# Row-wise start of a fused MLP kernel, with two roundings of h moved to GpSimd

## What is computed

```python
h = jax.nn.gelu(jnp.einsum('bnd,hd->bnh', x, fc1_w) + fc1_b, approximate=False)
shared = jnp.einsum('bnh,sh->bns', h, fc2_w) + fc2_b
We = experts_w[indices]
be = experts_b[indices]
expert_x = jnp.einsum('bnh,bph->bnp', h, We) + be[:, None, :]
x + jnp.concatenate([shared, expert_x], axis=-1)
```

## Time and profile before

| | us |
|---|---|
| median of 3 runs | 360.57 |
| lowest, highest | 360.05, 361.18 |
| profiled execution | 360.29 |
| its span | 358.1 |
| TensorE busy | 352.4 (98%) |
| VectorE busy | 260.3 (73%) |
| ScalarE busy | 246.6 (69%) |
| GpSimd busy | 235.0 (66%) |

### The profile page before, as it was taken

How to read it: one execution, slowest core, us unless ns; L and a number is a source line. 1 busy time by engine, 2 the same in 40 slices (tenths; PEclk the granted TensorE clock), 3 DMA queues, 4 the chain that set the end, 5 groups by cost and what they waited for, 6 DMA issues and landing times.

```text
span 358.1 us, 7085 instructions
## 1 busy us (share of the span) xinstructions
PE 352.4 (98%) x2383; PEld 324.2 (91%) x2383; DVE 260.3 (73%) x500; ACT 246.6 (69%) x410; POOL 235.0 (66%) x150
## 2 busy tenths in 40 slices
PE   8999999999999999999999999999999999999995
PEld 6899899999999999999999999999999999999984
DVE  1797976977859698686968869697786959844543
ACT  3794957777677686776777678677767768656640
POOL 0079977858756587765758866586865658774570
PEclk9999999999999999999999999999999999999999
DMA  8969654524324333332533324234331231312001
GB/s 197 189 148 206 144 144 131 150 78 108 112 59 136 94 90 126 89 120 66 147 97 88 113 78 128 82 94 149 90 102 57 88 98 32 117 37 90 29 31 59
DMA packets 70061, 37.53 MB, mean 105 GB/s; under 512 B 43530, under 2 KB 70026, under 8 KB 70026
## 3 DMA queue, kind: packets, MB, share of 16 engines
q1 hardware_dynamic: 69408, 36.55, 38.0%
q10 hardware_dynamic: 618, 0.53, 0.6%
HBM read 28.68 MB, written 8.39 MB: 104 GB/s over the span
## 4 chain that ended last, share of the span: by engine, by line
PE 98%; DVE 0%; ACT 0%; issue 0%; POOL 0%; POOLq 0%; DVEq 0%
PE fc_ps L1091 39%; PE acc_ps L1147 30%; PE acc_ps L1150 15%; PE fc_ps L1067 6%; PE acc_ps L1117 3%; PE fc_ps L1036 2%; PE fc_ps L1147 1%; PE tr_ps L1030 1%; PE fc_ps L1150 1%; PE fc_ps L1074 1%; DVE resid L914 0%; ACT w1t L469 0%; PE acc_ps L1030 0%; POOL ident L416 0%; POOL ident L414 0%
## 5 line engine op out<-in xcount | busy, mean ns | idle before, releaser
L390 POOL TENSOR_TENSOR ht<-gelu,ht 128x1024 fp32r<-128x1024 f32 x62 | 149.5, 2412 | 98.8 <-ACT ht L560 98.8
L1147 PE MATMUL acc_ps<-w2t,ht 128*128 128x512 f32 x464 | 168.0, 396 | 0.0
L1091 PE MATMUL fc_ps<-xt,w1t 128*128 128x256 f32 x1176 | 159.6, 283 | 0.0
L1091 PEld LDWEIGHTS fc_ps<-xt,w1t 128*128 128x128 f32 x1176 | 148.6, 189 | 5.3
L1150 PE MATMUL acc_ps<-w2t,ht 128*128 128x256 f32 x464 | 130.0, 280 | 0.0
L1147 PEld LDWEIGHTS acc_ps<-w2t,ht 128*128 128x128 f32 x464 | 87.4, 188 | 16.0 <-POOL ht L390 0.3
L1150 PEld LDWEIGHTS acc_ps<-w2t,ht 128*128 128x128 f32 x464 | 87.8, 189 | 0.0
L560 ACT ACTIVATE ht<-gelu 128x1024 fp32r<-128x1024 f32 x64 | 68.0, 1063 | 3.3
L586 ACT ACTIVATE gelu<-work,b 128x512 f32<-128x512 f32 x56 | 37.3, 715 | 26.4 <-DVE work L865 26.2
L398 POOL TENSOR_TENSOR xt<-work,xt 128x1024 fp32r<-128x1024 f32 x14 | 33.8, 2415 | 14.9 <-ACT xt L549 14.9
L865 DVE TENSOR_TENSOR work<-fc_ps,work 128x512 f32<-128x512 f32 x28 | 19.4, 691 | 22.6 <-PE fc_ps L1091 21.3
(11 more groups left out here) (70 smaller groups left out, 326.6 us busy)
## 6 DMA issues: line engine op xcount, KB each, us to landing
pieces<-in_L_cond_experts_w SPq DMA_DIRECT2D x128, 64.0 KB, 2.0
out<-resid SPq DMA_DIRECT2D x32, 256.0 KB, 3.1
pieces<-in_x SPq DMA_DIRECT2D x60, 128.0 KB, 2.9
resid<-in_x SPq DMA_DIRECT2D x15, 512.0 KB, 3.5
e_bias<-in_L_cond_experts_b SPq DMA_DIRECT2D x32, 32.0 KB, 2.8
work<-in_L_cond_fc_w SPq DMA_DIRECT2D x4, 256.0 KB, 4.4
w_piece<-in_L_cond_fc_w SPq DMA_DIRECT2D x4, 192.0 KB, 5.2
resid<-in_x SPq DMA_DIRECT2D x2, 256.0 KB, 3.5
```

The source lines that it names most:

```text
L390: nc.gpsimd.tensor_tensor(ht[:, slot, LO, :, :].rearrange("p k t -> p (k t)"), gelu[:, q % GELUS, :, :].rearrange("p k t -> p (k t)"), ht[ ...
L1091: last = nc.tensor.matmul(fc1_ps[:, dst, j * SEQ:(j + 1) * SEQ], w1t[:, w, wv, ms], xt[:, n % 2, o, xv, :], start=(fresh and j == 0 and at ...
L1147: nc.tensor.matmul(acc.rearrange("p (v o) -> p v o", v=2), ht[:, q % SLOTS, HI, j, ts], w2t[:, :, k, fc2_columns(b)], start=(k == 0), stop ...
```

## The change

Three things change, all in the first part of the program.

Order by rows. Loads of fc1_w half 0 are made by pairs of chunks (`load_w1_pair`): pair 0 half on SP's and half on ScalarE's queue, pair 1 on SP's; row 1 of x moves to ScalarE's queue, and index and fc1's bias go behind it. Transposes of x are by row (`x0_banks(b)` gives one bank with both halves of the features), those of fc1_w by pair of chunks. Chunks 0 and 1 are multiplied by row of x (`first_chunk(c, b)`, six matmuls of 256 columns): chunk 0 row 0, chunk 1 row 0, then, behind the transposes of the second pair, row 1 of both. Chunk 2 comes before the transposes of half 1, chunk 3 behind them. The copy of fc1's bias stays behind the `w1_low` of half 0.

Warm matmuls: `WARM` is 12 for 20, and the second group (10) is gone.

Rounding of h: for pairs 0 and 1 of block 0, GpSimd copies gelu to fp32r (`early_pair`, ahead of each `pair_lo`), and ScalarE's `conv_high(0)` and `conv_high(1)` go. On VectorE, `w1_low(1, *)` moves behind the first two `w2_square`, and on ScalarE `conv_chunk(1)` (a gelu) between the two `w1_high(1, *)`.

VectorE's `x0_low(b)` and `w1_low(half, l)` follow ScalarE's in the same forms and are left out below.

```diff
@@ -33,8 +33,9 @@
     GELUS = 4
+    EARLY = 2
     SLOTS = 6
-    WARM = 20
+    WARM = 12
@@ -115,13 +116,32 @@
+        def x0_row(v, b):
+            return xt0[:, :, v, b * SEQ:(b + 1) * SEQ]
+        def x0_bank(b):
+            return tr_ps[:, b, :].rearrange("p (d t) -> p d t", d=D)
+        W1_ORDER = ((0, 1), (1, 0))
+        def w1_slots(half, l, v):
+            cols = slice(2 * half * P, (2 * half + 2) * P)
+            if l == 0:
+                return w1t[:, W_A11:W_A12 + 1, v, cols]
+            return w1t[:, W_A22:W_A21 + 1:W_A21 - W_A22, v, cols]
+        def w1_rows(half, l):
+            return (acc_ps, tr_ps)[half][:, l, :].rearrange("p (d c) -> p d c", d=D)
...
         stored = [sem(f"stored{n}") for n in range(2)]
-        w1_loaded = [sem(f"w1_loaded{n}") for n in range(2)]
+        w1_loaded = [sem(f"w1_loaded{n}") for n in range(3)]
         w1p_loaded = sem("w1p_loaded")
@@ -195,6 +216,13 @@
+        def wait_h_hi(engine, q):
+            if q < EARLY:
+                engine.wait_ge(early_hi, q + 1)
+            else:
+                engine.wait_ge(h_hi, q - EARLY + 1)
@@ -261,11 +289,15 @@
-        def load_w1(queue, half):
-            ks = slice(half * HALF, (half + 1) * HALF)
-            for q in range(Q):
-                queue.dma_start(w1_in[S * q:S * (q + 1), ks, :], w1_v[q][:, ks, :])\
-                    .then_inc(w1_loaded[half], 16)
+        def load_w1_pair(queue, l, strips):
+            for q in strips:
+                queue.dma_start(w1_in[S * q:S * (q + 1), 2 * l:2 * l + 2, :],
+                                w1_v[q][:, 2 * l:2 * l + 2, :]).then_inc(w1_loaded[l], 16)
+        def load_x0(queue, b):
+            ts = slice(b * T, (b + 1) * T)
+            queue.dma_start(resid[:, 0, ts, :], x_blocks[0][:, ts, :]).then_inc(x0_loaded[b], 16)
@@ -312,12 +344,14 @@
-            for b in range(R):
-                ts = slice(b * T, (b + 1) * T)
-                sp.dma_start(resid[:, 0, ts, :], x_blocks[0][:, ts, :]).then_inc(x0_loaded[b], 16)
+            load_x0(sp, 0)
+            load_w1_pair(sp, 0, (0, 1))
+            load_w1_pair(sp, 1, range(Q))
             sp.wait_ge(x0_loaded[0], 16)
-            load_w1(sp, 1)
+            for q in range(Q):
+                sp.dma_start(w1_in[S * q:S * (q + 1), HALF:K, :], w1_v[q][:, HALF:K, :])\
+                    .then_inc(w1_loaded[2], 16)
             for q in range(Q):
@@ -384,9 +418,15 @@
+            def early_pair(q):
+                pool.wait_ge(conv_gelu, 2 * q + 2)
+                nc.gpsimd.tensor_copy(
+                    ht[:, q % SLOTS, HI, :, :].rearrange("p k t -> p (k t)"),
+                    gelu[:, q % GELUS, :, :].rearrange("p k t -> p (k t)")).then_inc(early_hi, 1)
...
                 slot = q % SLOTS
-                pool.wait_ge(h_hi, q + 1)
+                wait_h_hi(pool, q)
                 nc.gpsimd.tensor_tensor(
@@ -418,6 +458,8 @@
             for r in range(PAIRS):
+                if r < EARLY:
+                    early_pair(r)
                 pair_lo(r)
@@ -451,22 +493,14 @@
         def _(act):
...
+            def x0_high(b):
+                act.wait_ge(x0_tr, b + 1)
+                nc.scalar.activation(x0_row(HI, b), x0_bank(b), ACT.Copy).then_inc(x0_hi, 1)
+            def w1_high(half, l):
+                act.wait_ge(w1_tr, 2 * half + l + 1)
+                nc.scalar.activation(w1_slots(half, l, HI), w1_rows(half, l), ACT.Copy)\
+                    .then_inc(w1_hi, 1)
@@ -607,9 +641,10 @@
+            load_w1_pair(act, 0, (2, 3))
+            load_x0(act, 1)
             act.dma_start(index_sb[:, :], index.rearrange("(o n) -> o n", o=1))\
                 .then_inc(index_loaded, 16)
-            load_w1(act, 0)
             act.dma_start(b1_in[:, :].rearrange("k (q c) -> k q c", q=Q),
@@ -618,27 +653,25 @@
             act.wait_ge(gelu_loaded, 1)
-            for d in range(D):
-                x0_high(d)
-            for d in range(D):
-                w1_high(0, d)
+            x0_high(0)
+            w1_high(0, 0)
+            x0_high(1)
+            w1_high(0, 1)
             act.wait_ge(b1_ready, 1)
...
             w1_high(1, 0)
+            conv_chunk(1)
             w1_high(1, 1)
-            conv_chunk(1)
             w2_high(0)
...
             w2_high(3)
-            conv_high(0)
             conv_chunk(4)
...
             conv_chunk(5)
-            conv_high(1)
             conv_chunk(6)
@@ -796,7 +821,7 @@
             def plain_low(q):
-                dve.wait_ge(h_hi, q + 1)
+                wait_h_hi(dve, q)
                 nc.vector.tensor_tensor(
@@ -913,16 +938,16 @@
-            for d in range(D):
-                x0_low(d)
-            for d in range(D):
-                w1_low(0, d)
+            x0_low(0)
+            w1_low(0, 0)
+            x0_low(1)
+            w1_low(0, 1)
             dve.wait_ge(b1_tr, 1)
             nc.vector.tensor_copy(b1[:, :], fc1_ps[:, 3, 0:K]).then_inc(b1_ready, 1)
-            for d in range(D):
-                w1_low(1, d)
             w2_square(0)
             w2_square(1)
+            w1_low(1, 0)
+            w1_low(1, 1)
             w2_low(0)
@@ -1038,17 +1063,15 @@
                 pe.wait_ge(x0_loaded[b], 16)
...
+                transposes(tr_ps[:, b, :], [
+                    feature_chunk(resid[:, 0, b * T + t, :], d)
+                    for d in range(D) for t in range(T)]).then_inc(x0_tr, 1)
+            def w1_bank(half, l):
+                k = half * HALF + 2 * l
+                transposes((acc_ps, tr_ps)[half][:, l, :], [
+                    feature_chunk(w1_in[:, k + j, :], d)
+                    for d in W1_ORDER[l] for j in range(2)]).then_inc(w1_tr, 1)
@@ -1069,19 +1092,24 @@
+            def first_chunk(c, b):
+                for at, (w, v, d) in enumerate([(w, v, d) for w, v in ((HI, HI), (HI, LO), (LO, HI))
+                                                for d in range(D)]):
+                    if c == 0 and at == 0:
+                        pe.wait_ge(w1_hi, 1)
+                        pe.wait_ge(x0_hi, b + 1)
+                    if c == 0 and (w, v, d) == (HI, LO, 0):
+                        pe.wait_ge(x0_lo, b + 1)
+                    if c == 0 and (w, v, d) == (LO, HI, 0):
+                        pe.wait_ge(w1_lo, 1)
+                    last = nc.tensor.matmul(fc1_ps[:, c, b * SEQ:(b + 1) * SEQ],
+                                            conv_operand(c, d, w),
+                                            xt0[:, d, v, b * SEQ:(b + 1) * SEQ],
+                                            start=(b == 0 and at == 0), stop=True,
+                                            skip_group_check=True)
+                if b == R - 1:
+                    last.then_inc(conv_filled, 1)
@@ -1158,25 +1186,29 @@
             warm(WARM)
-            for b in range(R):
-                x0_banks(b)
-            warm(WARM // 2)
+            x0_banks(0)
             pe.wait_ge(w1_loaded[0], 16 * Q)
-            for d in range(D):
-                w1_bank(0, d)
+            w1_bank(0, 0)
+            x0_banks(1)
+            first_chunk(0, 0)
             pe.wait_ge(b1_loaded, 16)
             nc.tensor.transpose(fc1_ps[:, 3, 0:K], b1_in[:, :], ident[0:K, 0:K]).then_inc(b1_tr, 1)
-            first_chunk()
+            first_chunk(1, 0)
             pe.wait_ge(w1_loaded[1], 16 * Q)
-            for d in range(D):
-                pe.wait_ge(x0_lo, d + 1)
-                w1_bank(1, d)
-            conv_chunk(1)
+            w1_bank(0, 1)
+            first_chunk(0, 1)
+            first_chunk(1, 1)
+            pe.wait_ge(w1_lo, 2)
             conv_chunk(2)
+            pe.wait_ge(w1_loaded[2], 16 * Q)
+            pe.wait_ge(x0_lo, 2)
+            for l in range(2):
+                w1_bank(1, l)
             conv_chunk(3)
-            pe.wait_ge(w1_lo, 4)
+            pe.wait_ge(w1_lo, 3)
             conv_chunk(4)
             conv_chunk(5)
+            pe.wait_ge(w1_lo, 4)
             conv_chunk(6)
...
```

More of the change, by code:

```diff
@@ L163, in cond_mlp_residual @@
         h_hi = sem("h_hi")
+        early_hi = sem("early_hi")
         b1_ready = sem("b1_ready")
@@ L700, in _, with x0_low, w1_low @@
         def _(dve):
[L701 to L717 removed]
+            def x0_low(b):
+                dve.wait_ge(x0_hi, b + 1)
+                nc.vector.tensor_tensor(x0_row(LO, b), x0_bank(b), x0_row(HI, b).bitcast(FP32),
+                                        ALU.subtract).then_inc(x0_lo, 1)
+            def w1_low(half, l):
+                dve.wait_ge(w1_hi, 2 * half + l + 1)
+                nc.vector.tensor_tensor(w1_slots(half, l, LO), w1_rows(half, l),
+                                        w1_slots(half, l, HI).bitcast(FP32), ALU.subtract)\
                     .then_inc(w1_lo, 1)
@@ L1040, in x0_banks @@
                 pe.wait_ge(x0_loaded[b], 16)
-                for d in range(D):
-                    last = transposes(tr_ps[:, d, b * SEQ:(b + 1) * SEQ],
```

(25 more changed lines are left out.)

31 lines of the change are left out of this document (removed).

## The result

The changed kernel takes 364.69 us (median of 6 runs, 363.17 to 365.88) against 360.88 for the kernel before in the same comparison (6 runs). The ratio is 1.0109, 95% interval 1.009 to 1.0129: 3.2 to 4.7 us slower, where I forecast 360.3 and a range up to 362.1.

The account below looks back on a forecast made before the run. TensorE's own sequence was taken as the bound. It alone gains 1.4 us, but waits for VectorE leave chunk 8 only 0.3 earlier, so the median of 360.57 becomes 360.3; range 359.2 to 362.1.

Parts of the forecast that it names:

- Nothing behind chunk 8 is changed on TensorE, and it has no wait there that the shift could absorb: TensorE after chunk 8: the gain of 0.3 at chunk 8's start carries through to the end.
- Part 2: fc1_w half 0 loaded by pairs over both queues: first pair lands at 4.9, between 4.55 and 5.3.
- Part 4: VectorE, fc1_w half 1 behind two fc2_w squares: a new wait, its chain from w2_low on 0.75 to 0.8 late.
- rival (b): TensorE's clock rises late, near 11: 1.85 later than forecast, 361.8 profiled, 362.1 on the median; chance 0.20.
- Part 6: GpSimd's copies of h: 2.4 each, hidden with cover of 1.8 and 1.6 us, costing VectorE's critical operations nothing.
- The copy's price: GpSimd's one-input copy of 1024 elements: between 0.29 and 2.41, taken as 2.4.
- Part 5: ScalarE without two roundings of h: 0.5 of VectorE's 0.65 of waits goes, chunk 8 starts 0.3 earlier.
- rival (c): First fc1_w pair lands after 5.6 us, behind x's rows; 0.5 to 1 late gives 360.6 to 361.3; chance 0.12.
- Part 1: 18 warm matmuls less at the start: 2.85 us leave TensorE, transposes of x's row 0 start at 4.1 to 4.2.
- Signs asked for: In the changed profile: chunk 4 not after 15.8, TensorE waits ahead of fc2_first(0) and chunk 8, w2_low near 15.4.

Follow-up runs that it names:

- a_psum: The changed kernel with block 2's x_low on VectorE reading its first operand from PSUM instead of the SBUF copy: 361.73 us, ratio 1.0036.
- b_late_xlow: The kernel before with one spare VectorE copy from PSUM put ahead of block 2's x_low: 363.32 us, ratio 1.0082.
- b_early: The kernel before with only GpSimd's rounding of pairs 0 and 1 of h in place of ScalarE's: 360.8 us, ratio 1.0009.
- a_act_round: The changed kernel with ScalarE again rounding pairs 0 and 1 of h instead of GpSimd: 363.08 us, ratio 1.0055.
- the pair with 20 warm matmuls: The changed kernel with block 2's x_low reading PSUM and 20 warm matmuls, without and with half 1's transposes ahead of chunk 2: 362.21 and 360.8 us.
- b_best: The kernel before with 12 and 6 warm matmuls, GpSimd's rounding, the PSUM operand and the index load behind fc1_w's half 0: 361.03 us, ratio 1.0017.
- b_warm12: The kernel before with 12 and 6 warm matmuls for 20 and 10, in the old order: 359.81 us, ratio 0.9974.
- a_half1_psum: The changed kernel with block 2's x_low reading PSUM and half 1's transposes ahead of chunk 2: 361.21 us, ratio 1.0026.
- b_warm12_only: The kernel before with 12 warm matmuls and no second group, in the old order: 359.77 us, ratio 0.9985.

## Why the prediction was wrong, step by step

- **"Nothing behind chunk 8 is changed on TensorE, and it has no wait there that the shift could absorb"** is the step that failed. It is true of the kernel before; the changed one has a wait of 1.60 at 46.7 and loses 0.65 more by 58 us. VectorE's first drain had a lead of 0.65 us over TensorE; it hung on GpSimd's sums of fc1_w, and these on a race of 0.03 us. Taking the race out gains 3.0 in the medians and 2.4 in the profiled pair (a_psum), 2.4 with 20 warm matmuls (364.63 and 362.21), and making it in the kernel before costs 2.65 (b_late_xlow). It is most of the 3.8. The other 1.06 (a_psum) is the late start, where I had a gain of 0.3: parts 2 and 4 and rival (b) below.
- **Part 6, "GpSimd's new work costs them nothing"**, was argued from VectorE operations with one input in PSUM, and for those it was right. I didn't look at operations with both inputs in SBUF. The Trainium skill (GPSIMD Engine Reference, Key points) names them, beside a 2-port mode of VectorE, as what contends with GpSimd for the SBUF interfaces that the two engines share. The traces agree: 256 columns took 2.62 beside GpSimd's pair_lo(3) with two SBUF inputs, and 0.41 at the same place with one in PSUM. It wasn't GpSimd's added work as such that did it, though (b_early is level with before), but that pair_lo(3) came 0.1 us sooner once ScalarE was relieved (a_act_round).
- **The copy's price** was bounded by 0.29 and 2.41, and I took 2.4. It took 1.04 and was hidden, as predicted. With ScalarE's rounding in its place fc2_first(0) waits 1.25 for pair_lo(0) (a_act_round).
- **Part 4, the new wait on VectorE.** The mechanism was right and its size wrong. The squares started at 13.02 (forecast 13.0 to 13.2), but w2_low at 17.30 instead of 15.4. I had half 1's transposes at 12.05 and they came at 14.34, and I held ScalarE's gelu between its two roundings to be free, while it cost 0.37. That the transposes come a whole chunk and more behind their place before is part of the change and costs about 1 by itself (the pair with 20 warm matmuls).
- **Part 5** was right: from w2_low to the end of x1_lo VectorE took 25.97 - 17.30 = 8.7, and I had 9.2 - 0.5.
- **Part 2** was 0.9 short. The first pair landed at 5.8, not 4.9, x's row 0 at 4.3. I had x's row 0 at 3.76, from the 3.0 that it took before; with loads issued on ScalarE's queue at the same time it took 3.5. In b_best, where fc1_w's loads likewise went first on ScalarE's queue, x's rows took 3.8 and 5.1, against 3.0 and 4.0 in b_warm12. That was rival (c), with 0.12.
- **Part 1 and rival (b).** The clock rose near 10.6 in the profiled execution. The rival was described rightly, and its price for TensorE's own work, 1.85, nearly so: a_half1_psum and a_psum are the same program up to row 1 of chunks 0 and 1. The first, whose clock rose near 5.2, came to it at 9.64, the second, with a rise near 10.9, at 11.28. That is 1.64, of which 0.2 lie in the landing of the first pair. The rival's 362.1 left out the race too. But neither it nor (c) is needed for the loss: with 20 warm matmuls the time was the same, 364.63.
- **Signs asked for.** Chunk 3 started at 15.20 and chunk 4 six matmuls behind it, at about 16.7. I had forecast 14.85 and said that anything behind 15.8, its start in the kernel before, would refute me. TensorE's waits at fc2_first(0) and chunk 8 are there too, 0.46 and 0.16, though 2 us later than forecast; what ended the first the profile doesn't name. So the start was wrong by my own rule, of which a_psum says that it is worth about 1 us of the median, and the rest is the race.

What stays open: why the clock rises near 5 in some executions and near 10.5 in others of kernels with the same beginning. Of the profiles of kernels in the new order with 12 warm matmuls, three had it between 10.3 and 10.9 (the changed kernel, a_psum, a_act_round) and one near 5.2 (a_half1_psum), whose program is the same up to there. The Trainium skill (TensorE: Matmul & The Clock Gate, PE-mode transpose) says that transposes don't count as a busy TensorE in the same way; that four or six matmuls in the gap took the late executions away fits that. It took two of ten in each of three comparisons (a_psum, a_half1_psum, b_warm12_only), and none of the 28 executions with them was late; but that the late ones were late by the clock is seen in one profile alone (a_psum), so it isn't shown. Against the page stand b_warm12, where the rise came under the transposes, within 1 us of the last warm matmul, and b_warm12_only, where it came over 2 us behind it with nothing but transposes between.
